# Writing a two-at-a-time loop out in full and giving four engines new order lists (RWKV mixing, latent attention, eight experts)

## The reference, cut to what matters

```python
# layer 1: RWKV mixing, a recurrence over time in each of 512 channels
k, r = xn @ Wk.T, xn @ Wr.T
out = sigmoid(r) * wkv_scan(-exp(time_decay), time_first, k, r)
x = x + out @ Wo.T
# layer 2: attention between the 16 heads of ONE token, then 8 experts, all of them used
q  = (h @ Wq + bq).reshape(b, t, 16, 32)
kv = ((h @ Wdown + bdown) @ Wup + bup).reshape(b, t, 16, 64)
k, v = jnp.split(kv, 2, axis=-1)
att = softmax(einsum('bthd,btgd->bthg', q, k) / sqrt(32))
x = x + (einsum('bthg,btgd->bthd', att, v).reshape(b, t, 512) @ Wo + bo)
gate = softmax(h2 @ Wg + bg)
x = x + einsum('btd,edf,bte->btf', h2, We, gate)
```

## Time and profile before

| | |
|---|---|
| median of 3 runs | 3222.83 us (3214.9 to 3233.78) |
| the profiled execution | 3235.43 us, its span 3233.6 us |
| busy in that span | PE 2904.1 us (90%), DVE 2221.2 (69%), ACT 1286.2 (40%), POOL 619.2 (19%) |
| granted TensorE clock, mean | 0.933 of full |

### The profile page before, as it was taken

How to read it: one execution, slowest core, us unless ns; L and a number is a source line. 1 busy time by engine, 2 the same in 40 slices (tenths; PEclk the granted TensorE clock), 3 DMA queues, 4 the chain that set the end, 5 groups by cost and what they waited for, 6 DMA issues and landing times.

```text
span 3233.6 us, 53881 instructions
## 1 busy us (share of the span) xinstructions
PE 2904.1 (90%) x18864; PEld 1822.3 (56%) x18864; DVE 2221.2 (69%) x4132; ACT 1286.2 (40%) x2399; POOL 619.2 (19%) x681
## 2 busy tenths in 40 slices
PE   2359999999999999999999999999999899999989
PEld 2236665655665655656565565556566565566644
DVE  4787777677666767767676766767766666776663
ACT  2354443433443434444343444444344343444421
POOL 0111122211212212112221121222111221212120
PEclk9669999898999989999998999999899999999999
DMA  6011221101121201121210111220112120212110
GB/s 198 16 18 27 34 34 27 31 24 28 27 34 28 34 21 27 27 34 27 34 31 24 27 27 28 34 34 23 26 27 34 28 33 21 34 21 34 27 20 14
DMA packets 588333, 102.96 MB, mean 32 GB/s; under 512 B 556562, under 2 KB 556690, under 8 KB 588050
## 3 DMA queue, kind: packets, MB, share of 16 engines
q1 hardware_dynamic: 588068, 99.40, 18.0%
HBM read 48.49 MB, written 16.78 MB: 20 GB/s over the span
## 4 chain that ended last, share of the span: by engine, by line
issue 63%; POOL 13%; PE 11%; DVE 7%; SPq 3%; ACT 2%; DMA 1%; POOLq 1%; DVEq 0%; ACTq 0%
PE bank L1080 8%; POOL k L498 2%; POOL x L493 2%; POOL qo L498 2%; POOL acc L520 2%; PE bank L1232 2%; POOL ev L484 2%; POOL zz L480 1%; DVE wkv L895 1%; SPq L442 1%; SPq L438 1%; DVE w_e L827 1%; DVE zz L919 1%; DVE mcol L991 1%; POOL rs L511 1%
## 5 line engine op out<-in xcount | busy, mean ns | idle before, releaser
L1080 PE MATMUL bank<-w_e,h2t 128*128 128x512 f16 x6144 | 1459.4, 396 | 25.8 <-DVE acc L1060 25.8
L1080 PEld LDWEIGHTS bank<-w_e,h2t 128*128 128x128 f16 x6144 | 617.8, 102 | 771.8 <-issue 109.6
L1060 DVE SCALAR_TENSOR_TENSOR acc<-bank,gates,acc 128x512 f32<-128x512 f32 x512 | 370.1, 733 | 173.8 <-PE bank L1080 173.8
L595 ACT ACTIVATE e<-v 128x512 f32<-128x512 f32 x64 | 40.5, 633 | 737.1 <-DVE wkv L895 737.1
L480 POOL TENSOR_TENSOR zz<-wkv,zz 128x512 f32<-128x512 f32 x64 | 105.3, 1645 | 1112.8 <-DVE ev L906 1112.8
L1232 PEld LDWEIGHTS bank<-vp,pr 128*128 128x128 f32 x2048 | 286.6, 214 | 12.8 <-issue 2.4
L1232 PE MATMUL bank<-vp,pr 128*128 128x33 f32 x2048 | 290.8, 292 | 1.9 <-ACT pr L661 1.9
L661 ACT ACTIVATE pr<-bank,col 128x512 f32<-128x512 f32 x256 | 172.5, 686 | 249.1 <-PE bank L1222 249.1
L1080 PE MATMUL bank<-w_o,xo 128*128 128x512 f16 x768 | 176.0, 387 | 78.9 <-DVE xo L857 78.9
L991 DVE TENSOR_REDUCE mcol<-bank 128x4 f32<-128x512 f32 x256 | 158.8, 682 | 114.2 <-PE bank L1213 114.2
L895 DVE TENSOR_TENSOR_SCAN wkv<-e,wkv 128x256 f32<-128x256 f32 x256 | 233.9, 955 | 2.0 <-ACT e L590 2.0
(11 more groups left out here) (177 smaller groups left out, 3678.7 us busy)
## 6 DMA issues: line engine op xcount, KB each, us to landing
qs<-qo SPq DMA_DIRECT2D x384, 64.0 KB, 3.4
xk<-in_attn_x SPq DMA_DIRECT2D x32, 512.0 KB, 3.6
x<-in_attn_x SPq DMA_DIRECT2D x32, 512.0 KB, 3.6
result<-acc SPq DMA_DIRECT2D x32, 512.0 KB, 2.8
ks<-k SPq DMA_DIRECT2D x128, 64.0 KB, 3.3
w_e<-in_ffn_We SPq DMA_DIRECT2D x7, 1024.0 KB, 13.5
qs<-m SPq DMA_DIRECT2D x256, 2.0 KB, 1.7
qs<-in_attn_Wk SPq DMA_DIRECT2D x1, 1024.0 KB, 5.5
```

What stands on the lines that cost most here:

```text
L1060: V.scalar_tensor_tensor(out=acc[:, s, :], in0=moe_bank[u % 2][:, :], scalar=gates[:, s, e:e + 1], in1=acc[:, s, :], op0=ALU.mult, op1=ALU ...
L1080: ins = nc.tensor.matmul(dst, left(a), right(b), start=(n == 0), stop=(n == last))
```

## The change

All 34 passes are written out, with no loop, and the lists of PE, DVE, ACT and POOL are replaced. SP's list stays. No instruction of a step is added, removed or changed, only its place; the register arithmetic and the jumps of the loop go. On PE: `moe` 0 stands ahead of `mix_turn`; `moe` 2 and 3 stand between `att_q` and `att_up`; `moe` 4 and 5 between `att_up` and `mix_v`; the four `att_max` steps stand together; and `moe` 9, 10 and 11 stand in three places among the score products (9 before `att_probs` 0, 10 after `att_scores` 4, 11 after `att_scores` 7), with `moe` 12 and 13 between `att_probs` 7 and `att_project`.

```diff
--- before.py
+++ after.py
@@ -130,40 +130,40 @@
 
 
 PE_ORDER = [
-    ("mix_turn", 0), ("moe", 0), ("moe", 1), ("att_turn", 0), ("mix_k", 0), ("att_latent", 0), ("att_q", 0),
-    ("att_up", 0), ("mix_v", 0), ("moe", 2), ("moe", 3), ("moe", 4), ("att_max", 0), ("att_max", 1), ("moe", 5),
+    ("moe", 0), ("mix_turn", 0), ("moe", 1), ("att_turn", 0), ("mix_k", 0), ("att_latent", 0), ("att_q", 0),
+    ("moe", 2), ("moe", 3), ("att_up", 0), ("moe", 4), ("moe", 5), ("mix_v", 0), ("att_max", 0), ("att_max", 1),
     ("att_max", 2), ("att_max", 3), ("moe", 6), ("moe", 7), ("moe", 8), ("att_scores", 0), ("att_scores", 1),
     ("moe", 9), ("att_probs", 0), ("att_scores", 2), ("att_probs", 1), ("att_scores", 3), ("att_probs", 2),
-    ("att_scores", 4), ("att_probs", 3), ("att_scores", 5), ("att_probs", 4), ("att_scores", 6), ("att_probs", 5),
-    ("att_scores", 7), ("moe", 10), ("att_probs", 6), ("att_probs", 7), ("moe", 11), ("moe", 12), ("att_project", 0),
-    ("moe", 13), ("moe", 14), ("moe", 15), ("att_turn2", 0), ("mix_project", 0), ("att_gate", 0),
+    ("att_scores", 4), ("moe", 10), ("att_probs", 3), ("att_scores", 5), ("att_probs", 4), ("att_scores", 6),
+    ("att_probs", 5), ("att_scores", 7), ("moe", 11), ("att_probs", 6), ("att_probs", 7), ("moe", 12), ("moe", 13),
+    ("att_project", 0), ("moe", 14), ("moe", 15), ("att_turn2", 0), ("mix_project", 0), ("att_gate", 0),
 ]
 
 DVE_ORDER = [
-    ("att_stats", 0), ("att_norm", 0), ("mix_turn", 0), ("moe_gate", 0), ("att_turn", 0), ("att_latent", 0),
-    ("mix_decay", 0), ("moe", 0), ("moe", 1), ("att_stack", 0), ("moe", 2), ("att_vt", 0), ("moe", 3), ("mix_sum", 0),
-    ("mix_value", 0), ("moe", 4), ("att_max", 0), ("att_max", 1), ("att_max", 2), ("att_max", 3), ("att_m", 0),
-    ("moe", 5), ("mix_scan", 0), ("moe", 6), ("mix_rec", 0), ("moe", 7), ("mix_rec", 1), ("mix_gate", 0), ("moe", 8),
-    ("mix_split", 0), ("att_probs", 0), ("att_probs", 1), ("moe", 9), ("att_probs", 2), ("att_probs", 3),
-    ("mix_decay", 1), ("att_probs", 4), ("att_probs", 5), ("moe", 10), ("att_probs", 6), ("att_probs", 7),
-    ("att_back", 0), ("mix_sum", 1), ("mix_value", 1), ("moe", 11), ("moe", 12), ("mix_scan", 1), ("att_project", 0),
-    ("mix_rec", 2), ("moe", 13), ("mix_rec", 3), ("mix_gate", 1), ("moe", 14), ("mix_split", 1), ("pre_stats", 0),
-    ("moe", 15), ("pre_norm", 0), ("att_turn2", 0), ("mix_project", 0),
+    ("att_stats", 0), ("att_norm", 0), ("mix_turn", 0), ("moe_gate", 0), ("att_turn", 0), ("moe", 0), ("moe", 1),
+    ("mix_decay", 0), ("moe", 2), ("att_latent", 0), ("moe", 3), ("att_stack", 0), ("moe", 4), ("moe", 5),
+    ("att_vt", 0), ("att_max", 0), ("att_max", 1), ("att_max", 2), ("att_max", 3), ("att_m", 0), ("moe", 6),
+    ("mix_sum", 0), ("mix_value", 0), ("moe", 7), ("mix_scan", 0), ("mix_rec", 0), ("mix_rec", 1), ("moe", 8),
+    ("att_probs", 0), ("att_probs", 1), ("mix_gate", 0), ("moe", 9), ("att_probs", 2), ("mix_split", 0), ("moe", 10),
+    ("att_probs", 3), ("mix_decay", 1), ("att_probs", 4), ("att_probs", 5), ("moe", 11), ("att_probs", 6),
+    ("mix_sum", 1), ("att_probs", 7), ("att_back", 0), ("moe", 12), ("moe", 13), ("mix_value", 1), ("mix_scan", 1),
+    ("mix_rec", 2), ("att_project", 0), ("mix_rec", 3), ("mix_gate", 1), ("mix_split", 1), ("moe", 14), ("moe", 15),
+    ("att_turn2", 0), ("pre_stats", 0), ("mix_project", 0), ("pre_norm", 0),
 ]
 
 ACT_ORDER = [
-    ("mix_turn", 0), ("att_norm", 0), ("moe_gate", 0), ("att_turn", 0), ("mix_k", 0), ("moe", 0), ("moe", 1),
-    ("att_latent", 0), ("att_q", 0), ("att_up", 0), ("mix_v", 0), ("moe", 2), ("moe", 3), ("mix_exp", 0), ("moe", 4),
-    ("moe", 5), ("moe", 6), ("moe", 7), ("mix_num", 0), ("att_rest", 0), ("att_scores", 0), ("moe", 8), ("moe", 9),
-    ("att_scores", 1), ("mix_split", 0), ("att_scores", 2), ("att_scores", 3), ("att_scores", 4), ("att_scores", 5),
-    ("att_scores", 6), ("att_scores", 7), ("moe", 10), ("mix_exp", 1), ("att_back", 0), ("moe", 11), ("moe", 12),
-    ("mix_num", 1), ("moe", 13), ("att_square", 0), ("att_norm2", 0), ("moe", 14), ("moe", 15), ("mix_split", 1),
-    ("att_turn2", 0), ("pre_norm", 0),
+    ("mix_turn", 0), ("att_norm", 0), ("moe_gate", 0), ("att_turn", 0), ("moe", 0), ("moe", 1), ("mix_k", 0),
+    ("moe", 2), ("moe", 3), ("att_latent", 0), ("att_q", 0), ("att_up", 0), ("moe", 4), ("moe", 5), ("moe", 6),
+    ("mix_v", 0), ("att_rest", 0), ("mix_exp", 0), ("moe", 7), ("moe", 8), ("att_scores", 0), ("att_scores", 1),
+    ("mix_num", 0), ("att_scores", 2), ("att_scores", 3), ("moe", 9), ("mix_split", 0), ("att_scores", 4),
+    ("moe", 10), ("moe", 11), ("att_scores", 5), ("att_scores", 6), ("att_scores", 7), ("mix_exp", 1),
+    ("att_back", 0), ("moe", 12), ("moe", 13), ("moe", 14), ("moe", 15), ("mix_num", 1), ("att_square", 0),
+    ("att_norm2", 0), ("mix_split", 1), ("att_turn2", 0), ("pre_norm", 0),
 ]
 
 POOL_ORDER = [
-    ("att_stats", 0), ("moe_acc", 0), ("att_q", 0), ("att_up", 0), ("mix_sum", 0), ("mix_num", 0), ("mix_sum", 1),
-    ("att_rest", 0), ("mix_num", 1), ("att_square", 0), ("moe", 15), ("pre_stats", 0),
+    ("att_stats", 0), ("moe_acc", 0), ("att_q", 0), ("att_up", 0), ("mix_sum", 0), ("mix_num", 0), ("moe", 15),
+    ("att_rest", 0), ("mix_sum", 1), ("mix_num", 1), ("att_square", 0), ("pre_stats", 0),
 ]
 
 SP_ORDER = [
@@ -359,12 +359,7 @@
                     steps[name](Tile(0, 0, 0), k)
             if between:
                 between()
-            for i in range(4):
-                iteration(i, i % 2, i // 2)
-            with eng.Fori(0, (NT - 6) // 2) as pair:
-                for par in range(2):
-                    iteration(pair * 2 + (4 + par), par, pair + 2)
-            for i in range(NT - 2, NT + 2):
+            for i in range(NT + 2):
                 iteration(i, i % 2, i // 2)
 
         weight_dram = {"k": wk, "r": wr, "o1": wo1, "q": wq, "o2": wo2}
```

## The result

The changed kernel takes **3008.16 us** (median of 4 runs, 3005.85 to 3008.79) against 3228.31 of the kernel before (4 runs, 3214.9 to 3236.66): a ratio of 0.932, 95% interval 0.9284 to 0.9356. It is faster by 6.8%. Execution against profiled execution, as the sum was made, it is 3235.4 to 3007.6, -228 where -125 was forecast.

What follows compares the result with a forecast made beforehand. The prediction took PE, with its waits and slow clock, to bound the kernel. Its terms summed to -125 us, from the earlier kernel's median of 3222.8 to 3098 us, with a range of 3045 to 3165.

Steps and rivals of the forecast that it cites:

- jumps, with their clock: At the loop's twelve jumps: 5.5 us each of standing still and slow clock would go, -66 us.
- `att_max` in one piece: Four `att_max` steps together: PE waits for DVE's reductions, 3.3 us instead of 1.8, +39 us.
- wait for m: Ahead of `att_scores` 0: PE arrives before m's DMAs are done, 0.7 us a pass, +18 us.
- clock at `att_max`: Around `att_max`: the slow clock mostly goes, keeping 0.2 of 1.2 us a pass, -26 us.
- clock at the score products: Among the score products: `moe` 10 and 11 cut the narrow run, keeping 0.6 of 2.6 us a pass, -52 us.
- waits of the tail: Behind `att_probs` 7: `att_turn2` waits 1.4 us and `mix_project` 0.8, against 0.76 together before, +39 us.
- front: Start of attention: DVE's `pre_norm` now precedes `att_stats`, delaying `att_turn` by 0.45 us a pass, +12 us.
- passes 0 to 3 and 30 to 33: Passes outside the loop: smaller waits lost, the same new ones, one expert step more cover, together -8 us.
- The first: Score products: the clock falls in the shorter pieces too, giving back 52 us or more, 3150 us; chance 0.15.
- The third: Start of score products: POOL's L493 holds `mix_rec` 0 and 1, making DVE late, +62 us, 3160 us; chance 0.10.
- The fourth: Straight code: instructions not fetched in time, one stall of 5.5 us in every pass gives 3285 us; chance 0.03.
- The second: New waits smaller than worked out: scans not held, m in time, no clock lost, about 3035 us; chance 0.12.

Runs made afterwards that it cites:

- e1: Kernel before with its old lists, all 34 passes written out and nothing else changed: 3149.75 us, ratio 0.9762.
- e2: Changed kernel with its new lists, but the old loop kept for passes 4 to 29: 3095.98 us, ratio 0.96.
- e7: Changed kernel with `moe` 6 moved between `att_max` 1 and 2 on PE, and earlier on DVE: 3111.95 us, ratio 0.9651.
- e6: Changed kernel with POOL's `att_rest` back behind `mix_sum` 1, beside the scans: 3049.21 us, ratio 0.945.
- e9: Changed kernel with DVE's `mix_value` 1 moved ahead of `moe` 12 and 13: 2978.17 us, ratio 0.9231.
- e4: Changed kernel with `moe` 10 behind `att_scores` 5 on PE and behind `att_probs` 3 on DVE: 3027.76 us, ratio 0.9384.
- e3: Changed kernel with `mix_gate` 0, `mix_split` 0 and `mix_decay` 1 later on DVE and ACT, PE's list unchanged: 3128.23 us, ratio 0.9695.

## Why the prediction was right or wrong

The terms, the measured ones read from the stretches and waits above and times 26 or 25 as there:

| term | forecast | measured | from |
|---|---|---|---|
| jumps, with their clock | -66 | -67 | 115.6 + 57.4 - 106.3 |
| wait for `ks` | -68 | -67 | 67.7, now 2.8; with the 26th pass |
| waits for `acc` and `t` | -26 | -26 | neither is left |
| `att_max` in one piece | +39 | +36 | 3.2 us instead of 1.8 |
| wait for m | +18 | +22 | 21.3/25 x 26 |
| clock at `att_max` | -26 | -31 | none left |
| clock at the score products | -52 | -67 | 302.4, now 302.7 with 2.6 x 26 of work more |
| waits of the tail | +39 | +4 | (11.3 + 11.1)/25, was 0.76 |
| front | +12 | 0 | no wait ahead of `att_turn` |
| small ones and clock in the tail | +13 | about 0 | what is left over |
| passes 0 to 3 and 30 to 33 | -8 | -31 | 740.1, now 709.0 |
| sum | -125 | -227 | of -228 |

- **The mechanisms in the looped passes were right, and the sizes of six terms were not.** The first five terms are off by 4 us at most, and no term has the other sign, though two came to nothing. The missing 102 us are the tail (35), the clock kept back (29), the passes outside (23) and the front (12), and some 3 of the small ones. `e1` and `e2` tell the loop's part from the lists', and `e7` shows that `att_max` in one piece buys the short wait for m.
- **The tail, "+1.5, +39 us", was sized wrongly, by 35.** The chain was the right one: `att_back` ended 5.0 us after `att_probs` 7 (5.2 forecast), the scans were held for 0.9 us beside L475 (1.1), the last leg took 3.2. But the sum gave `x2` at E + 13.9 and it came at E + 12.9 (1367.35 - 1354.43). From start to start the steps measure 4.9 for `att_back`, 1.3 for `moe` 12 and 13, 1.3 for `mix_value`, 2.4 for the scans with the copy behind them and 1.7 for `mix_rec` 2, and 1.3 for the additions to `x2`; the sum had 5.2, 1.4, 1.3, 2.7, 1.74, 1.41 and 0.15 of gaps. So each step was sized a little long. Durations of records had been added up, with gaps on top, where a DVE record overlaps the start of the next by up to 0.1 us: that is some 0.4 of the 1.0. The rest is `att_back` 0.2 earlier, the scans held 0.2 less, and the additions 0.1 shorter. It came off whole at `att_turn2` (a wait of 0.45 instead of 1.4) and by 0.35 more at `mix_project` (0.45 instead of 0.8). Against a wait of 1.4 us, an error of 1.0 is most of it. `e6` and `e9` show that this chain does set the wait: longer by 1.0, it costs 41 us, shorter by 0.9, it gives 30.
- **The clock kept back was 29 too much**: "I keep 0.2" (5), "I keep 0.6" (16) and the tail's clock (8). Over the score products the clock did not fall a little less; it did not fall at all, in any of 26 passes. `e4` shows how near it is: with 1 us more in a run it is below full in 6 passes.
- **The passes outside, "together -8", were off by 23.** Passes 2, 3, 30 and 31 went from 368.2 to 353.7 us: in passes 2, 30 and 31 they too had paid the slow clock at the score products, 3.3 us each (pass 31: 93.7 us, now 88.6), and I had priced only their waits. Pass 3 stood at full clock before, too. Passes 0 and 1 went from 181.8 to 172.8; they are 171.8 in `e2` and 181.4 in `e1`, so that is the lists' doing, in passes where DVE also cuts weights. Which step of the lists was not tried. The last two went from 129.8 to 122.4 us. The score stretch of pass 31 in the kernel before:

```profile
3060.10:3072.50 12.40, 12.40 (x85) 10.27 (x85) 6.86 (x20) 6.72 (x12) 0.00 (x0) 0.72 0.01 3
```

- **The front, "+0.45", +12, measured 0.** There was indeed no slack: `att_turn` follows `att_norm` at once in both. But the delay was mis-sized. What now stands ahead of `att_stats` is one DVE instruction of 0.15 us, and `att_stats` starts 0.74 us after the last addition to `x` instead of 0.66 (1378.26 - 1377.52 and, in pass 10, 1092.64 - 1091.98): 0.08 and not 0.45. It is this one:

```profile
1378.19 0.15 DVE L865 SCALAR_TENSOR_TENSOR nb<-mv,rs 128x2 f32<-128x2 f32 x1
```

- **The rivals.** The first (clock falls in the shorter pieces too) fell: 1.00 in 26 of 26. The third (L493 holds the reciprocals) fell: 1730 ns. The fourth fell: straight code shows no "issue" wait of PE at all. (The page that the prediction names for the jump, the Trainium skill's "Runtime: NRT & Kernel Launch", section "Instruction fetch mechanics", doesn't leave the cost of straight code open, as the prediction has it: it calls the cost of crossing a block of instructions "mostly hidden", and this trace agrees.) The second comes nearest in number, and that is luck: the clock was not lost, which is 23 of its 69 us, but the scans were held and m did wait, which are the other 46. Its own terms sum to 3029 and not 3035. The three clock sizes were each chosen on the careful side, and such choices add up in one direction.
- **The rule weighed.** The Trainium skill, page "SBUF — State Buffer", section "Who interferes with whom", let the scans be held and the reciprocals not, by their number of SBUF inputs. The timelines agree: scans at 2.27 and 3.24 us beside POOL additions and 1.38 alone, reciprocals at 1730 ns beside L488. POOL is held too: the two additions of L488 took 3.26 us beside the scans in `e6` and 2.50 beside reciprocals in pass 14 of the changed kernel.

## What to carry to other kernels

Where PE's narrow products run back to back, look at the clock of the stretch in every pass before looking at waits: wide steps moved into the middle gave back 67 us here, as much as the longest wait, and they add no work. Add up a chain from start to start, not by the durations of records, when the wait at its end is as short as the error can be. And ask of a wait for small DMAs how long their issue takes: two queues may remove it.

## What was not expected of the hardware

- The clock falls with no gap in PE's work: with runs of 33-column and score products of 3.3, 4.3 and 6.5 us it was below full in 0, 6 and 21 of 26 passes. After a wait of 3.3 to 3.9 us the full-width products behind it were slow too (`e3`: 7.0 us instead of 5.3; `e7`: 4.44 instead of 2.75).
- A backward jump costs 3.15 us of standing still and 4.55 with its clock in `e2`; and with the loop, the waits for the stacking DMAs are 17 us longer than without it, for the same lists, and in 12 of 26 passes the clock falls behind them.
- Issuing eight small DMAs took 5.0 us, 0.62 each; two queues took 2.5 us side by side.
